# K and V rows of five tiles loaded row by row by SyncE instead of by GpSimd's gathers, in a graph attention kernel

## What is computed

```python
Q, K, V = x @ Wq + bq, x @ Wk + bk, x @ Wv + bv          # 6250 x 96 each, as 8 heads of 12
E = edge_attr @ We + be                                  # 100000 x 96
score = K[src] * Q[dst] / sqrt(12) * E
score = exp(clip(score.sum(over the 12), -5, 5))         # one number per edge and head
wV = segment_sum(V[src] * score, dst)
Z = segment_sum(score, dst)
out = layernorm(x + wV / (Z + 1e-6))
```

## Time and profile before

| | before |
|---|---|
| median of three runs | 1006.52 us (1005.41 to 1007.03) |
| the profiled execution | 1005.39 us |
| its span, first to last instruction | 1003.7 us |
| POOL busy | 746.0 us, 74% |
| DVE busy | 651.0 us, 65% |
| PE busy | 640.7 us, 64% |
| ACT busy | 185.3 us, 18% |
| moved by DMA | 165.50 MB, 165 GB/s |

### The profile page before, as it was taken

The page is one execution under the profiler, slowest core; times in us unless marked ns, Lnnn a source line. Parts: engine busy times, 40 slices in busy tenths (PEclk is TensorE's granted clock), DMA queues, the critical chain, the costliest instruction groups (busy, mean ns, idle before and its releaser), DMA issues. The chain is left out here.

```text
span 1003.7 us, 11961 instructions
## 1 busy us (share of the span) xinstructions
PE 640.7 (64%) x3276; PEld 416.9 (42%) x3276; DVE 651.0 (65%) x1307; ACT 185.3 (18%) x368; POOL 746.0 (74%) x788
## 2 busy tenths in 40 slices
PE   6778778574866665576556656664566457646664
PEld 5655555343533443344334434433334234434443
DVE  6638998576656665676466656665666567647665
ACT  4742222111111111111111111111111111111111
POOL 7777777777777777777777777777777777777772
PEclk9889998888677777777778777778778777787885
DMA  6999877655565556546655575566556654665531
GB/s 200 314 284 243 211 205 192 169 152 152 154 166 142 147 151 185 147 135 179 168 138 163 136 185 146 137 175 175 136 147 154 184 146 135 177 161 136 136 92 42
DMA packets 101368, 165.50 MB, mean 165 GB/s; under 512 B 45164, under 2 KB 63885, under 8 KB 101293
## 3 DMA queue, kind: packets, MB, share of 16 engines
q1 hardware_dynamic: 63117, 84.39, 30.9%
q0 software_dynamic: 37024, 75.35, 28.7%
q10 hardware_dynamic: 1152, 4.92, 1.3%
HBM read 152.18 MB, written 12.39 MB: 164 GB/s over the span
## 5 line engine op out<-in xcount | busy, mean ns | idle before, releaser
L390 POOL DMA_INDIRECT kv<-kv_table,idx x750 | 713.2, 951 | 228.5 <-issue 227.6
L492 PE MATMUL psT<-identity,qe 96*128 96x96 f32 x782 | 113.3, 304 | 306.1 <-DVE qe L826 306.0
L906 DVE TENSOR_TENSOR qke<-psT,kv 128x768 f32<-128x768 f32 (+1 forms) x99 | 93.5, 944 | 296.4 <-DMA kv<-kv_table,idx 294.5
L471 PE MATMUL psE<-ea,we 97*96 97x512 f32 x392 | 260.8, 802 | 0.8 <-ACT kv L611 0.8
L492 PEld LDWEIGHTS psT<-identity,qe 96*128 96x128 f32 x782 | 91.4, 175 | 322.0 <-DVE qe L826 321.8
L541 PEld LDWEIGHTS psA<-place,msg 128*104 128x104 f32 x1536 | 159.2, 179 | 40.6 <-DVE msg L933 33.1
L541 PE MATMUL psA<-place,msg 128*104 128x104 f32 x1536 | 168.1, 264 | 11.5 <-DVE msg L933 11.3
L641 ACT ACTIVATE qe<-psE 96x1024 f32<-96x1024 f32 (+1 forms) x99 | 99.9, 1009 | 226.1 <-PE psE L471 226.1
L826 DVE TENSOR_TENSOR qe<-psQ,qe 96x1024 f32<-96x1024 f32 (+1 forms) x99 | 118.6, 1198 | 6.5 <-ACT qe L641 6.4
L655 ACT ACTIVATE msg<-clipped 128x64 f32<-128x64 f32 (+1 forms) x99 | 25.3, 255 | 526.1 <-DVE clipped L921 526.1
L471 PEld LDWEIGHTS psE<-ea,we 97*96 97x96 f32 x392 | 76.1, 219 | 80.8 <-issue 80.8
(11 more groups left out here) (104 smaller groups left out, 323.6 us busy)
## 6 DMA issues: line engine op xcount, KB each, us to landing
ea<-eaT SPq DMA_DIRECT2D x99, 384.0 KB, 4.4
q_parts<-rel_table SPq DMA_DIRECT2D x99, 252.0 KB
kv<-kv_table,idx POOLq DMA_INDIRECT x750
qwin<-q_table SPq DMA_DIRECT2D x198, 23.6 KB
xb<-xrows SPq DMA_DIRECT2D x24, 144.0 KB, 4.7
out<-ob SPq DMA_DIRECT2D x24, 144.0 KB
kv_table<-kv ACTq DMA_DIRECT2D x2, 960.0 KB, 8.4
q_table<-q_parts SPq DMA_DIRECT2D x2, 720.0 KB, 4.8
```

Source lines behind the costliest of these rows:

```text
L390: pool.indirect_dma_start(kv[:, k, t], None, kv_table, sources).then_inc(kv_in[k], 16)
L471: last = nc.tensor.matmul(psE[0:D, h, 0:size], we[:], ea[:, k % EAR, edge:edge + size], start=True, stop=True)
L492: last = nc.tensor.transpose(psT[:, t % 2, t // 2 * D:(t // 2 + 1) * D], qe[0:D, k % 2, t * P:(t + 1) * P], identity[0:D, 0:D])
L906: nc.vector.tensor_tensor(qke[:, 0:nt].rearrange("p (t b) d -> p b t d", **by_bank), psT[:, :, 0:nt // 2 * D].rearrange("p b (t d) -> p b ...
```

## The change

The last tile (t = 7) of groups 24, 40, 56, 72 and 88 is no longer gathered by POOL. A new input `src_row` holds the 5 x 128 source nodes of these tiles in one row; SP loads it at the start into `row_id`. In turns 7 to 86 SP reads eight of these numbers into registers and issues eight DMAs, each of which brings one row of `kv_table` into one partition of `kv_rows`; sixteen turns fill a tile, and the last turn for group 24 is turn 22. In the turn of the group before (23, ...) ACT waits for all 128 rows and for the ring slot, and copies the tile into `kv`. DVE waits for that copy ahead of its first product of the group; it and POOL count one gather less.

```diff
+BY_ROW = (24, 40, 56, 72, 88)
+ROWS = 8
...
+                        sp.dma_start(row_id[:], src_row).then_inc(row_id_in, 16)
                     sp.wait_ge(tables_up, 1)
...
+                    def load_single_rows(turn):
+                        i, j = turn // (P // ROWS), turn % (P // ROWS)
+                        if turn == 0:
+                            sp.wait_ge(row_id_in, 16)
+                            sp.wait_ge(kv_out, 16 * len(KV_CHUNKS))
+                        nodes = nc.values_load_multi_w_load_instructions(
+                            row_id[0:1, i * P + j * ROWS:i * P + (j + 1) * ROWS], engines=[sp.engine], min_val=0,
+                            max_val=N - 1, skip_runtime_bounds_check_because="source nodes of edges are nodes")[1]
+                        for p in range(ROWS):
+                            sp.dma_start(kv_rows[j * ROWS + p:j * ROWS + p + 1, i], kv_table[bass.ds(nodes[p], 1), :]
+                                         ).then_inc(rows_in[i], 16)
...
                         if j == 1 and at >= 2 * BG:
                             store_rows(q - 2, half, at)
+                        turn = at - (BY_ROW[0] - P // ROWS - 1)
+                        if 0 <= turn < len(BY_ROW) * P // ROWS:
+                            load_single_rows(turn)
...
                         for t in range(tiles(at)):
+                            if first and alone(at, t):
+                                continue
...
                         if at + 2 < NG:
                             edges_up(r, k + 2, at + 2)
+                        if first and at + 1 in BY_ROW:
+                            i = BY_ROW.index(at + 1)
+                            act.wait_ge(rows_in[i], 16 * P)
+                            act.wait_ge(msg_done, at + 1 - U + 1)
+                            nc.scalar.activation(kv[:, (at + 1) % U, T - 1], kv_rows[:, i], ACT.Copy).then_inc(rows_up, 1)
...
-                            dve.wait_ge(kv_in[k], 16 * (T * fills - (T - nt)))
+                            singles = sum(1 for x in BY_ROW if first and x <= at and x % U == k)
+                            dve.wait_ge(kv_in[k], 16 * (T * fills - (T - nt) - singles))
+                            if first and at in BY_ROW:
+                                dve.wait_ge(rows_up, BY_ROW.index(at) + 1)
```

More of the change, by code:

```diff
@@ L57, in lap, with gnn_program @@
     return (U // ring) * r + k // ring + 1
-def gnn_program(nc, xT, xrows, src, dst_group, dst_tile, eaT, w_node, w_edge, out):
+def gnn_program(nc, xT, xrows, src, src_row, dst_group, dst_tile, eaT, w_node, w_edge, out):
     f32, bf16, i32 = mybir.dt.float32, mybir.dt.bfloat16, mybir.dt.int32
@@ L126, in gnn_program @@
         ea = sb("ea", [DA, EAR, GE], f32)
+        row_id = sb("row_id", [1, len(BY_ROW) * P], i32)
+        kv_rows = sb("kv_rows", [P, len(BY_ROW), 2 * D], f32)
         qwin = sb("qwin", [P, QRING, 2, D], bf16)
@@ L168, in gnn_program @@
         turned, turned_up, conv_mm, conv_up = sem("turned"), sem("turned_up"), sem("conv_mm"), sem("conv_up")
+        row_id_in, rows_up = sem("row_id_in"), sem("rows_up")
+        rows_in = [sem(f"rows_in{i}") for i in range(len(BY_ROW))]
         kv_in = [sem(f"kv_in{i}") for i in range(U)]
@@ L196, in tiles, with alone @@
             return TAIL_TILES[at - NB] if at >= NB else T
+        def alone(at, t):
+            return at in BY_ROW and t == T - 1
         def engine_turns(eng, body, unrolled):
@@ L397, in _ @@
                         missing = (T - TAIL_TILES[s]) if s < len(TAIL_TILES) else 0
+                        missing += sum(1 for at in BY_ROW if first and at % U == s)
                         pool.wait_ge(kv_in[s], 16 * (T * groups - missing))
@@ L1053 @@
         "src": np.ascontiguousarray(src_pad.reshape(NG * T, P).T),
+        "src_row": np.concatenate([src_pad[at, (T - 1) * P:T * P] for at in BY_ROW])[None],
         "dst_group": dst_pad,
```

## The result

The changed kernel takes 999.18 us (median of six runs, 998.97 to 999.58), the kernel before 1006.22 us in the runs beside it (six, 1005.41 to 1007.43). The ratio is 0.9928, with an interval of 0.9918 to 0.9938: 7.0 us less, between 6.2 and 8.3. The forecast was 1000.3 us, 6.25 us less.

The account below looks back on a forecast made before the run. POOL's beat of gathers was taken as the bound. Five gathers fewer gave 6.25 us and all added work was charged nothing: 1006.52 - 6.25 = 1000.3 us, range 997.4 to 1003.2 us.

Parts of the forecast that it names:

- POOL's beat: POOL's gathers of K and V: 0.946 us plus 0.30 us issue, 1.25 us each; five fewer gain 6.25 us.
- The path is charged nothing: SP's added 5.04 us a turn, 403 us in 80 turns, fits its 492.8 us of waits; 90 us left.
- The row's pitch: SP's issue and address operation for one single-row transfer: 0.50 us, between 0.47 and 1.43.
- The register load: SP's load of eight row numbers ahead of each turn's transfers: 1.04 us.
- The thin place early on: SP's turns 7 to 15: falls behind 2.4 us a turn, 19 us, covered by leads and POOL's 14.1 us of room.
- The hand-over a few us late: ACT's copy for group 24 comes a few us late; DVE makes it up and it does not reach POOL.
- the leads: SP's loads are asked for ahead of use: 14 us at the early pace, 25 us at the full one.
- ACT's copy: ACT's five copies of 128x192 tiles: 0.3 to 1.0 us each, at most 5 us, hidden in its waits.
- The excess of gathers: Gather time beyond 0.946 us each, 3.7 us before; assumed the same, with -2.3 to +2.3 us of change.
- SP as the bound: Rival: above 0.64 us a row SP's turns outlast POOL's beat; 1063 us at 0.80 us a row; chance 0.08.
- Each row waits for the one ahead to land: Rival: SP's row loads run one after another, 19.0 us a turn, 1680 us in all; chance 0.02.
- The rows slow the gathers: Rival: row transfers lengthen each of some 620 gathers by 10 ns, 6.2 us back, 1006.5 us; chance 0.07.

Follow-up runs that it names:

- padded: Against the kernel with seven tiles row by row: row numbers laid out so each turn's eleven begin at a multiple of 64 bytes; 996.37 us, ratio 0.9906.
- seven tiles: Against the changed kernel: seven tiles loaded row by row in place of five, eleven rows a turn over twelve groups each; 1018.47 us, ratio 1.0112.
- ten tiles: Against the changed kernel: ACT's queue also brings the last tile but one of the five groups, eight rows a turn; 994.73 us, ratio 0.9879.
- fifteen tiles: Against the changed kernel: ACT also brings two more tiles for each of the five groups, sixteen rows a turn; 1028.92 us, ratio 1.0221.

## Why the prediction was right, point by point

- **POOL's beat bounds the time; each gather is worth 1.25 us.** Right. With 2, 5, 7 and 10 gathers taken away the time fell by 3.17, 5.9 to 7.1 (six medians), 9.96 and 11.69 us, against 2.5, 6.25, 8.75 and 12.5; with the gathers left in, by 0.68 with an interval that holds no change. The traces show it more sharply. From the first gather's start to the last one's end, less what gathers take beyond 946 ns each, lie 937.7 us in both kernels with 750 gathers, 935.2 with 748, 931.4 to 931.5 in all six with 745 that SP does not bind, 929.0 with 743 (padded) and 925.2 with 740: 1.25 us for each gather.
- **The path is charged nothing.** Right: with rows 999.63 us, without them 999.60; and four further transfers in each turn changed nothing.
- **The row's pitch, 0.50 us between 0.47 and 1.43.** Too high: 0.41, of which 0.23 is the issue. The window load that it was taken from has 126 pieces, and even the lightest transfer shown, 0.29 us, is more than a single row needs. **The register load, 1.04 us.** Too high: some 0.70, of which 0.63 is the load; I had taken the whole gap with a bound test and an address. Both errors went to the safe side: 5.04 us a turn were forecast, 4.0 were taken, and of SP's wait 172.7 us were left, not 90.
- **The thin place early on.** Right: 44.5 us of wait fell to 5.0, and SP fell behind from turn 7 on. The lag reached 14.8 us, in turn 17, where 19 us in turn 15 had been forecast; a turn took 4.0 us more, not 5.04. By turn 24 SP had drawn level. The kernel with twelve transfers a turn, 9.2 us of own work, had a lag of 24.8 us, and it was free.
- **The hand-over a few us late.** Wrong: the last row was issued 19.8 us ahead of the copy. The description of the loads and the prediction had read SP's turns one too late. Turn `at` of SP waits for the query matmul of group `at`, not `at + 1`: that of group 14 ends at 152.46, and turn 14, counted on from turn 6, begins its first load 0.2 us later (first line below). So the rel load at 239.00 belongs to turn 23; that of turn 22 ends at 225.41 (second line), 14 us earlier. The 80 turns end where turn 87 begins, at 876.31 us, and not at 889. For the same reason the loads are used four turns after they are asked for, not about three, and the leads are longer than the 14 and 25 us of the prediction. The cover behind the hand-over was real: 3.5 us of late copy in the kernel with twelve cost nothing.

```profile
152.69 0.88 SPq L234 DMA_DIRECT2D qwin<-q_table  x2
...
225.00 0.41 SPq L218 DMA_DIRECT2D q_parts<-rel_table  x1
```

- **ACT's copy, 0.3 to 1.0 us.** 0.35.
- **The excess of gathers, within 2.3 us of before.** 709.8 - 745 x 0.946 = 5.0 us after, 3.7 before, and from 3.2 to 5.6 in the other kernels with five gathers less. It took 1.3 us of the profiled execution's gain; the first gather, which starts at 44.91 us before, 43.70 after and between 43.4 and 46.0 in the experiments, gave 1.2 back.
- **The rest.** The measured 7.0 us are 0.8 more than five beats. The interval (6.2 to 8.3) just holds five beats, and the start's scatter is as large; the kernel that keeps all gathers also came out 0.68 us lower. The 0.8 us do not lie in the beat, which gave 6.2 to 6.3 us by the traces. Whether some of them are a real gain at the start or the end is open.
- **SP as the bound.** The mechanism is real, and in time it lies where it was forecast: 0.64 us a row makes 3.6 + 1.04 + 8 x 0.64 = 9.8 us of work in a turn. Turns of 9.2 us (twelve transfers) and 9.3 us (seven tiles, padded) were free, turns of 10.1 and 10.9 us were not. Since a row takes 0.41 us, in transfers it lies further off, between twelve and sixteen, or one misplaced register load of eleven numbers. The leads, put at 39 us with POOL's room, took 42 us with sixteen transfers and 31 with seven tiles; that 39 came out so near is in part luck, since it read the lead a turn too short.
- **Each row waits for the one ahead to land.** Ruled out: 640 rows at a pitch of 0.41 us, while a row has landed 1.4 to 1.8 us after its issue began (seven tiles), sooner than by the 2.0 us that the prediction quotes. The Trainium skill, page "DMA: Bandwidth & Descriptors", section "Rules for kernel authors", would have small transfers joined into one large one, since those under 64 KB are mostly overhead. The traces agree, as half rows go at the same 0.41 us as whole ones, but here it is overhead of a queue that waited, put in the place of 1.25 us per tile on the one that did not.
- **The rows slow the gathers.** Ruled out: a median of 946 ns with and without them, and no loss in the kernel that has both.

The Trainium skill says in the same section that spreading transfers over several engines' queues brings no bandwidth and saves only the issuing engine's time. With ten tiles that time was all that was wanted: 994.73 us, 11.69 us less. No run here tests the bandwidth.

## What to carry to other kernels

Where one engine's issue rate sets the time, a few of its operations can be moved to a queue that waits, even at forty times the engine time (128 x 0.41 us on SP for 1.25 us of POOL's), as long as that queue's waits in the very stretch, and not on average over the run, exceed what is added; a lag early on is free as long as the leads cover it. Price the unit of the moved work by the smallest operation in the trace and expect less. The engine to watch next need not be the one with the fullest total; here it was the one between two steps of the chain: ACT broke with some 8 us of work in a turn, SP only where its turn of 10.1 us exceeded the 9.5 us that a turn has in this stretch (758.7 / 80).

## What had not been expected of the hardware

- SP's register load depends on how many numbers it loads and where they lie: eight aligned ones 0.63 us, eleven aligned to 64 bytes 1.40 us, eleven at offsets that are no multiple of 16 bytes 2.3 to 2.8 us. On ACT sixteen took 1.20 us. What in the load makes the difference was not looked into.
- A DMA of one row of 768 bytes is issued in 0.23 us by SP and, in the kernels with ten and fifteen tiles, at a median pitch of 0.39 us by ACT; half rows go at the same pitch, 16 transfers in 6.46 us.
- SP can be 24.8 us late behind the matmul that it awaits without any effect on the end.
